# A two-layer transformer block on one core: new places, banks and end rounds for all pieces, and a query and key split in two halves

## The reference

```
x = x + LN(attn0(LN(x)));  x = x + LN(ffn0(LN(x)))
x = x + LN(attn1(LN(x)));  x = x + LN(ffn1(LN(x)))

attn0: 16 heads of 16; q, k, v = x W.T + b; RoPE on q and k; causal softmax(q k.T / 4) v; out W.T + b
ffn0:  h = silu(x Wg.T) * (x Wu.T), 768 wide; h Wd.T     (weights are integers / 127)
attn1: 16 heads of 64; sim = q k.T / 8; sim = 50 tanh(sim / 50); causal softmax(sim) v; out Wo.T
ffn1:  xr, xk = mixes of x and x shifted by one token; sigmoid(xr Wr.T) * (relu(xk Wk.T)**2 Wv.T)
```

## Time and profile before

| | |
|---|---|
| median of three runs | 1496.42 us (1495.2 to 1499.88) |
| profiled execution | 1490.64 us |
| its span | 1488.8 us, mean granted TensorE clock 0.994 of full speed |
| TensorE matmuls busy | 1402.8 us (94%) |
| VectorE busy | 1082.9 us (73%) |
| ScalarE busy | 800.0 us (54%) |
| GpSimd busy | 788.5 us (53%) |
| DMA | 61.40 MB, mean 41 GB/s |

### The profile page before, as it was taken

How to read it: one execution, slowest core, us unless ns; L and a number is a source line. 1 busy time by engine, 2 the same in 40 slices (tenths; PEclk the granted TensorE clock), 3 DMA queues, 4 the chain that set the end, 5 groups by cost and what they waited for, 6 DMA issues and landing times. The chain is left out here.

```text
span 1488.8 us, 32925 instructions
## 1 busy us (share of the span) xinstructions
PE 1402.8 (94%) x12438; PEld 1042.0 (70%) x12438; DVE 1082.9 (73%) x2067; ACT 800.0 (54%) x1135; POOL 788.5 (53%) x994
## 2 busy tenths in 40 slices
PE   5889999999999998999999999999999999999996
PEld 4566767676767675777777777767677677677775
DVE  7888888888888877755567585585685665765766
ACT  2555444444444445555766656656556666566652
POOL 4344434444444442444666575666575565766652
PEclk8999999999999999999999999999999999999999
DMA  5221212112020122100100000010100100100001
GB/s 182 83 86 48 72 58 73 58 58 70 36 78 25 67 80 100 43 29 29 65 2 1 15 29 2 1 44 1 43 1 1 43 1 1 43 1 30 2 1 43
DMA packets 36547, 61.40 MB, mean 41 GB/s; under 512 B 3760, under 2 KB 19024, under 8 KB 36432
## 3 DMA queue, kind: packets, MB, share of 16 engines
q1 hardware_dynamic: 35568, 59.09, 11.4%
q10 hardware_dynamic: 864, 0.66, 0.2%
HBM read 25.86 MB, written 8.42 MB: 23 GB/s over the span
## 5 line engine op out<-in xcount | busy, mean ns | idle before, releaser
L1740 ACT ACTIVATE l_probs<-psum 128x1024 f32<-128x1024 f32 (+1 forms) x192 | 164.5, 879 | 165.2 <-PE psum L2074 127.8
L929 ACT ACTIVATE l_probs<-psum 128x512 f32<-128x512 f32 x256 | 138.3, 593 | 175.2 <-PE psum L1195 165.8
L321 POOL TENSOR_SCALAR_AFFINE_SELECT l_probs<-l_probs 128x256 f32<-128x256 f32 (+1 forms) x384 | 179.4, 498 | 0.0
L1012 DVE TENSOR_REDUCE l_rowmax<-psum 128x2 f32<-128x1024 f32 (+2 forms) x192 | 158.9, 862 | 20.4 <-PE psum L1156 19.8
L1836 DVE TENSOR_TENSOR l_qk_lo<-psum,l_qk_hi 128x1024 fp32r<-128x1024 f32 x64 | 77.6, 1218 | 117.0 <-ACT l_qk_hi L1730 116.5
L2117 PE MATMUL psum<-l_probs,l_v 128*32 128x512 f32 (+3 forms) x2048 | 151.8, 434 | 11.6 <-DVE l_qk_lo L1836 9.8
L1746 ACT ACTIVATE l_probs<-l_probs 128x2048 f32<-128x2048 f32 (+1 forms) x128 | 160.4, 1274 | 1.3
L1845 DVE RECIPROCAL l_keysum<-psum 128x256 f32<-128x256 f32 x64 | 112.3, 1754 | 44.0 <-PE psum L2103 37.4
L2117 PEld LDWEIGHTS psum<-l_probs,l_v 128*32 128x32 f32 x2048 | 65.5, 110 | 92.8 <-issue 80.2
L316 POOL TENSOR_TENSOR l_pool_holder<-expo 128x1 f32<-128x1 f32 x128 | 26.2, 204 | 195.5 <-ACT l_probs L1746 130.0
L1858 DVE TENSOR_TENSOR l_att<-psum,l_keysum 64x256 f32<-64x256 f32 x256 | 107.8, 421 | 15.9 <-PE psum L2117 9.1
(11 more groups left out here) (240 smaller groups left out, 4134.8 us busy)
## 6 DMA issues: line engine op xcount, KB each, us to landing
l_kT<-l_roped_hi SPq DMA_DIRECT2D x32, 256.0 KB, 2.7
l_qT<-l_roped_hi SPq DMA_DIRECT2D x32, 256.0 KB, 2.5
x_mid<-l_x SPq DMA_DIRECT2D x8, 516.0 KB, 2.7
l_x<-x_mid SPq DMA_DIRECT2D x8, 516.0 KB, 3.3
...
```

The source lines that it names most:

```text
L321: nc.gpsimd.affine_select(out=part, in_=part, compare_op=ALU.is_ge, fill=0.0, base=0, pattern=[[0, part.shape[1]], [1, P]], channel_multip ...
L929: space.free(nc.scalar.activation(probs[:, SLOT[p], e, c0:c1], space.unit(*use), ACT.Exp, scale=HD0 ** -0.5), *use)
L1012: reduced = nc.vector.tensor_reduce(rowmax[:, a // 2, :, a % 2, t], space.unit("max", a, k)[:, :, c0:c0 + (t + 1) * P], mybir.AxisListType ...
L1740: space.free(nc.scalar.activation(probs[:, p % 2, :, c0:c1], space.unit("score", p, u)[:, :, 0:c1 - c0], ACT.Tanh, scale=HD1 ** -0.5 / CLA ...
```

## The change

All tables are new: the pieces' times (`table`, `moved_table`) in both layers, the order of the weights' loads and splits, and the banks. The set of pieces is the same but for one thing: `qk_hi p` and `qk_lo p` are each one instruction over 128x1024 before, and two over 128x512 now. The first takes the queries, as soon as the 6 matmuls of the queries are done (a new semaphore, `qk_first`), the second takes the keys once the other 6 matmuls are done. The bank of the pair's projection is freed by the second `qk_lo`, as before. That is 64 more instructions on ScalarE and 64 more on VectorE. Below, the lines of the tables that the prediction speaks of (of some 250 that changed), and the whole of the change outside the tables.

```diff
 # layer 1, table
-        "x4_stats": {(): 50.401},
+        "x4_stats": {(): 47.741},
-        "x4_rstd": {(): 52.383},
+        "x4_rstd": {(): 48.712},
-        "x4_norm": {(): 51.224},
+        "x4_norm": {(): 52.099},
 # layer 1, bank_table
-        "qk": {(0,): 0, (1,): 2, (2,): 0, (3,): 4, (4,): 2, (5,): 2, (6,): 4, (7,): 2},
+        "qk": {(0,): 0, (1,): 4, (2,): 0, (3,): 4, (4,): 2, (5,): 2, (6,): 4, (7,): 2},
     shifted_ready = sig("shifted_ready", 1)
     x4_normed = sig("x4_normed", NT)
     x4_ready = sig("x4_ready", 1)
-    proj_hi = sig("proj_hi", NP1)
+    proj_hi = sig("proj_hi", 2 * NP1)
+    qk_first = sig("qk_first", NP1)
     exped = sig("exped", 2 * NP1)
     masked = sig("masked", 3 * NP1)
     summed = sig("summed", 3 * NP1)
 
         def projected(i, p):
             if p >= 2:
-                space.all_filled(act, i, [("qk", p)] + [("score", p - 2, u) for u in range(len(UNITS1))])
+                space.all_filled(act, i, [("score", p - 2, u) for u in range(len(UNITS1))])
+                act.wait_ge(qk_first.sem, qk_first.at(i, p + 1))
             else:
                 if started(i):
                     space.all_filled(act, i - 1, [("score", p - 2 + NP1, u) for u in range(len(UNITS1))], back=1)
-                space.filled(act, i, "qk", p)
-            nc.scalar.activation(qk1[0][:, p % 2, :, :], space.unit("qk", p), ACT.Copy).then_inc(proj_hi.sem, 1)
+                act.wait_ge(qk_first.sem, qk_first.at(i, p + 1))
+            nc.scalar.activation(qk1[0][:, p % 2, 0, :], space.unit("qk", p)[:, 0, :], ACT.Copy).then_inc(proj_hi.sem, 1)
+            space.filled(act, i, "qk", p)
+            nc.scalar.activation(qk1[0][:, p % 2, 1, :], space.unit("qk", p)[:, 1, :], ACT.Copy).then_inc(proj_hi.sem, 1)
 
         def score(i, p, u):
 
         def projected(i, p):
-            dve.wait_ge(proj_hi.sem, proj_hi.at(i, p + 1))
-            space.free(nc.vector.tensor_tensor(qk1[1][:, p % 2, :, :], space.unit("qk", p), qk1[0][:, p % 2, :, :].bitcast(F32),
-                                                ALU.subtract), "qk", p)
+            for b in range(2):
+                dve.wait_ge(proj_hi.sem, proj_hi.at(i, 2 * p + b + 1))
+                low = nc.vector.tensor_tensor(qk1[1][:, p % 2, b, :], space.unit("qk", p)[:, b, :],
+                                              qk1[0][:, p % 2, b, :].bitcast(F32), ALU.subtract)
+            space.free(low, "qk", p)
 
             weights.split(pe, i, 6)
             for b, w in enumerate((wq[:2], wk[:2])):
                 last = width_major(nc, space.unit("qk", p)[:, b, :], xT, w, slice(p * P, (p + 1) * P), NC)
+                if b == 0:
+                    last.then_inc(qk_first.sem, 1)
             space.fill(last, "qk", p)
 
         def score(i, p, u):
```

More of the change, by code:

```diff
@@ L604, in phase1 @@
[L604 to L605 removed]
+        "load_x": {(): -15.319},
+        "x_stats": {(): -18.194},
+        "x_rstd": {(): -22.344},
+        "x_norm": {(): -17.22},
+        "x_T": {(0,): -13.659, (1,): -12.596},
+        "x_T_hi": {(0,): -9.127, (1,): -9.12},
+        "x_T_lo": {(0,): -12.303, (1,): -12.14},
+        "rope": {(0,): -7.674, (1,): -4.98, (2,): 0.001, (3,): 4},
@@ new lines, in phase1 @@
+        "roped": {(0,): -8.605, (1,): -6.14, (2,): -0.179, (3,): 4.411},
+        "turned": {(0,): -6.156, (1,): -1.94, (2,): 1.536, (3,): 4.779},
+        "rope_sum": {(0,): -8.306, (1,): -2.88, (2,): -0.549, (3,): 1.2},
+        "rope_hi": {(0,): 0.714, (1,): 1.819, (2,): 10.747, (3,): 11.088},
+        "rope_lo": {(0,): -5.469, (1,): -2.077, (2,): 1.716, (3,): 2.001},
+        "place": {(0,): 1.911, (1,): 8.633, (2,): 18.456, (3,): 15.926},
+        "v": {(0,): 9.867, (1,): 10.245},
+        "v_out": {(0,): 14.138, (1,): 14.813},
@@ new lines, in phase1 @@
+        "o_stats": {(): 37.091},
+        "o_rstd": {(): 36.857},
+        "residual": {(): 42.459},
+        "o_norm": {(): 37.818},
+        "x1_stats": {(): 38.26},
+        "x1_rstd": {(): 39.429},
+        "x1_norm": {(): 39.636},
+        "gate": {(0,): 44.145, (1,): 44.8, (2,): 48.256, (3,): 49.306, (4,): 50.214, (5,): 51.733},
+        "tanh": {(0,): 44.75, (1,): 49.549, (2,): 52.277, (3,): 52.616, (4,): 55.616, (5,): 56.388},
+        "gated": {(0,): 41.858, (1,): 44.211, (2,): 48.237, (3,): 49.537, (4,): 50.909, (5,): 52.507},
@@ L669, in phase1 @@
+        "residual": {(0,): -20.577, (1,): 68.869, (6,): 184.732, (7,): 235.814},
+        "store": {(0,): 68.782, (5,): 184.554, (6,): 222.194, (7,): 289.306},
     }
@@ L1387, in phase2 @@
-        "mask": {(0,): 4.247, (1,): 4.515, (2,): 5.35, (3,): 8.092, (4,): 12.337, (5,): 22.428, (6,): 23.018, (7,): 27.04},
-        "sum": {(0,): 4.451, (1,): 4.74, (2,): 7.54, (3,): 8.093, (4,): 13.859, (5,): 22.528, (6,): 23.165, (7,): 27.476},
-        "den": {(0,): 10.802, (1,): 12.369, (2,): 15.385, (3,): 17.828, (4,): 20.812, (5,): 25.102, (6,): 28.873, (7,): 30.54},
-        "recip": {(0,): 3.48, (1,): 7.76, (2,): 15.07, (3,): 15.13, (4,): 16.56, (5,): 21.83, (6,): 26.797, (7,): 26.93},
@@ new lines, in phase2 @@
+        "mask": {(0,): 11.119, (1,): 11.638, (2,): 18.222, (3,): 19.226, (4,): 19.84, (5,): 20.25, (6,): 25.058, (7,): 28.809},
+        "sum": {(0,): 11.47, (1,): 12.613, (2,): 18.501, (3,): 19.227, (4,): 19.844, (5,): 23.241, (6,): 27.676, (7,): 34.226},
+        "den": {(0,): 10.588, (1,): 11.682, (2,): 15.431, (3,): 17.626, (4,): 20.546, (5,): 25.31, (6,): 28.588, (7,): 29.668},
+        "recip": {(0,): 8.195, (1,): 12.57, (2,): 13.463, (3,): 15.722, (4,): 15.729, (5,): 24.244, (6,): 27.442, (7,): 28.1},
@@ L1503, in phase2 @@
+        "load_x": {(0,): 210.853, (1,): 226.082, (2,): 291.091, (3,): 292.463},
+        "residual": {(0,): 291.028, (1,): 305.775, (2,): 320.671, (7,): 502.811},
+        "store": {(0,): 292.489, (1,): 312.376, (6,): 469.571, (7,): 521.743},
+        "store_b": {(7,): 547.83},
     }
```

451 lines of the change are left out of this document (211 added, 240 removed), and 9 rows, old and new, of the table moved_table.

## The result

The kernel after takes 1454.85 us (median of 4 runs, 1454.64 to 1455.65), the kernel before 1495.81 us (median of 4, 1491.91 to 1499.88). The ratio is 0.9727, with a 95% interval of 0.970 to 0.9753: 41 us faster. The forecast was 1471 us with a range from 1459 to 1488. The direction was right, the size was not.

A forecast was written before the change was run, and what follows sets the result against it. It took TensorE as the bound, busy 1402.8 of 1488.8 us, so only idleness could be won. From the profiled 1490.6, -14 -6 -4 gave 1466.6 us; with most of the profile-to-median distance added, 1471 us, range 1459 to 1488.

The forecast's parts named there:

- Part 3: Layer 0's looped rounds: the 1.2 us wait for rmax behind x_norm goes; -1.0 us a round, -4 in all.
- Part 1: Layer 1's looped rounds: reordering the norm's pieces and qk_lo 6 wins 3.5 us a round, -14 in all.
- the named waits: Layer 1's loop: TensorE's waits for qk_lo, 2.46 us ahead of pv 0 and 1.0 for qk_lo 6, both go.
- The new wait: Layer 1's loop: qk 2 waits for att 7, now behind the norm; 0 to 1.1 us, taken as 0.7.
- I carry about this distance over: From profiled execution to median: the 5.8 us by which before's median exceeds its profile is nearly kept, giving 1471 us.
- Part 2: Where the layers meet: SP's new queue order removes the 4.76 us maxima wait and low clock; -6 us, bounds -8 and +1.
- Part 4: The split of qk_hi and qk_lo: extra 14 us ScalarE, 12 us VectorE lie beside TensorE; 0, lower bound -5 us.
- Part 5: The start, layer 1's unrolled rounds and the end: no wait plainly removed or made; 0, bounds -6 and +6 us.
- The first rival: Layer 1's loop: the norm takes 6.7 us, not 3.1, at its new place, cancelling that gain; 1485 us, chance 0.12.
- The third rival: ScalarE held mid-qk_hi delays tanh and exp; 0.7 us a pair at TensorE costs 45 us, 1516 us; chance 0.06.

The follow-up runs named there:

- two_numbers: Kernel before with two numbers of layer 1's looped rounds changed: x4_rstd earlier on GpSimd, recip 3 behind qk_lo 6; median 1478.2 us, ratio 0.9886.
- filler: Kernel before with nine extra useless matmuls in each looped round of layer 1, where TensorE waits ahead of pv 0; median 1495.18 us, ratio 0.9979.
- few: Kernel before with eight numbers changed: those of `two_numbers` and `sp_order`, and layer 0's x_norm behind the next rmax; 1471.19 us, ratio 0.9831.
- xnorm_early: Kernel after with one number changed: x_norm one rmax earlier on VectorE in layer 0's looped rounds; 1458.84 us.
- sp_order: Kernel before with five numbers changed, giving SP's queue where the layers meet the order of after; median 1492.7 us, ratio 0.9975.
- norm_old: Kernel after with the last norm's pieces at their old places in layer 1's loop: x4_rstd behind mask 0, x4_norm behind att 7; 1511.69 us, ratio 1.0089.
- norm_old_xs: `norm_old` with x_stats moved back on VectorE, behind qk_lo 3, recip 0 and o_norm; 1458.76 us.
- split_only: Kernel before with only the split of qk_hi and qk_lo into halves, tables as before; 1496.18 us, ratio 0.9986.
- nosplit: Kernel after with qk_hi and qk_lo whole again, tables as after; 1455.69 us, ratio 0.9733 against before.
- norm_behind: Kernel after with one number changed: x4_norm behind att 7 in layer 1's looped rounds; 1455.45 us.

## Why the prediction was wrong

The forecast missed by 16 us. They add up, layer 1 counted by like rounds: 6.1 in layer 1's loop, 5.9 in layer 0's, 1.7 in the unrolled parts, 4.2 in the step from the profile to the median, less 1.8 where the layers meet.

- **The steps that failed.** The first two are of one size. Part 3, "I take -1.0 a round", where 2.3 was measured for layer 0's loop. It counted the one named wait of 1.2 us and left the other 2.3 us of idleness as they were, on the argument that VectorE is nearly full. VectorE was busy 65.98 us before and is 65.33 now, in a round that is 2.3 us shorter: at the 85% of before it was not the bound. x_norm's place gave 0.6 to 1 us of it. The rest came from waits for `exp` and masks that the prediction never listed: the rows above have 7.8 us of them in four rounds before, and 3.6 us of other waits after.
- Part 1, "I take half of it as gone", for layer 1's loop: 5.0 us a round instead of 3.5. The mechanism of the named waits was right. Both went, and `two_numbers` shows them at 3.7 us a round. The new wait ahead of qk 2 came as worked out, 0.46 us for 0.7. Too small was the rest: 1.1 of the 1.4 us of small waits went, not half, and 0.85 us of busy time went too, for which the sum had no term.
- Third: "I carry about this distance over". The 5.8 us between before's profile and its median were taken for a property of the measurement. They are a property of the kernel. Behind TensorE's waits the clock falls in some executions and not in others, and behind those of 2.5 us it costs 1.3 to 1.5 us each time; before's profile caught a run in which layer 1's loop was spared. After has no such waits in its loops: its four runs lie within 1.0 us, 0.2 us from the profile. The granted clocks of before's 63 runs say that its spread goes with the clock; which waits it falls behind is shown in part: `filler` took away the falls in layer 1's loop, and the median by 2.7 us, but left 7 us of spread. And it is no rule without exception: `few` and `xnorm_early` have no wait of 2 us in their loops, and one run of four 7 to 8 us above the others, at a lower clock.
- Part 2, where the layers meet: 4.2 us for 6. The wait of 4.76 us went, and the clock is at 1.00 in those ten microseconds, but small waits of 0.2 to 0.8 us came in. `sp_order` gives the same 4 us alone, though its clock did fall there.
- Part 4, the split at nothing: right, by two kernels from both sides. ScalarE's busy time grew by 7 us, not 14; a half takes 598 ns here, where 622 was taken.
- Part 5 put the unrolled rounds at 0 within 6; by like rounds they gave 1.7 us, and no run takes them apart. The end, whose 11.7 us of idleness the prediction named, gave nothing once the work that moved out of it is counted.
- The first rival, the norm at double length: it did not happen at the new place (3.06 us), and in `norm_old`, where it did, the length was not what cost. There the norm took 7.5 us, with GpSimd's sums and masks beside it: its four 128x256 instructions 4.64 us instead of 1.38. The Trainium skill, "SBUF — State Buffer", on who interferes with whom, has a VectorE instruction in a two-port mode, or with two SBUF inputs beside a GpSimd instruction that reads SBUF, contend with GpSimd for an exclusive lock. The trace agrees: 128x4 with two SBUF inputs takes 1.25 us in place of 0.16, and ends just as GpSimd's `att_lo` of 1.30 us does (1168.53 and 1168.51). By that rule alone 12 us a round would not have been forecast, and `norm_old_xs` shows 0.8 for the lateness and the length together.
- The third rival, ScalarE held in the middle of a pair, is refuted by `split_only` and `nosplit`. Its threshold was also a little low: the forecast stood 25.4 us below before's median, not 24, so it would have decided from 0.47 us a pair on, not 0.45.

What the prediction did not see at all is what the norm's end releases. It argued with `qk_lo 2` behind the norm. In the new order `x_stats` stands ahead of `qk_lo 2`, so the norm's end starts a chain of store, residual and load of which VectorE itself waits for the last link. That chain, not the norm's length, decides in the new order once the norm is late, and nothing in the forecast had a term for it. The norm's own place matters little: behind `att 7` the kernel takes as long (`norm_behind`). The place of `x4_rstd` on GpSimd does: behind mask 0 it turns 41 us of gain into 14 of loss.
